# Loads in another order, the preparation of the second attention moved into the second step, and permutations copied by VectorE

## The chip, the cores and the metric

The kernel is written in Bass for one NeuronCore of one Trainium2 chip: every engine has its own instruction stream, written out by hand, and the streams wait for each other by semaphores. The metric is the device time of one execution in microseconds (us), and the number that counts is the median of several runs. A shorter time is better.

## The reference

Two layers on x of 16 batches x 128 rows x 128 columns, with a context of 16 batches x 77 rows x 128 columns. All is float32.

```python
x = x + tanh(g_xattn[0]) * L0_xattn(ctx, layernorm(x), mask, ...)   # 16 heads of 64, keys are [ctx rows, x rows]
x = x + tanh(g_ffn[0])   * L0_ffn(layernorm(x), ...)                # linear, 9 butterfly stages, gelu, 9 butterfly stages, linear
x = x + tanh(g_xattn[1]) * L1_xattn(layernorm(x), ctx, Wq, Wk, Wv, Wo, bq, bk, bv, bo)  # 16 heads of 8, top 32 of 77 keys
x = x + tanh(g_ffn[1])   * L1_ffn(layernorm(x), Wr, br, W1, W2)     # each row goes to one of 8 experts

# a butterfly stage, s = 2**stage: pairs i and i+s of the 512 hidden columns are mixed by a 2x2 matrix each
# second attention, what does not depend on x:
K = ctx @ Wk.T + bk ;  V = ctx @ Wv.T + bv ;  result @ Wo.T + bo
```

## The kernel before

**Stages.** A preparation, then a pipeline of steps over the 16 batches, then a last stage over 23 tiles of 128 rows sorted by expert. A step has eight slots (0 to 7). In one step six different batches are at work, each in another phase: P and A (first attention), A2 (its end and the butterfly FFN), B, C and E (second attention and router). Each engine has a function `step(i, at)` that lists its work slot by slot, so the order of work on an engine is fixed by hand. Steps 0 to 5 and the last ones are written out; the middle ones are one loop. Step 0 holds only the start of batch 0 (its P phase): POOL normalises the inputs (`stage_inputs`, semaphore p_step, slot 1), TensorE (PE) transposes them in slot 6 (`keys_T`), ScalarE (ACT) copies them out, and PE makes the first keys and queries (`keys_in`, `queries_in`). Step 1 is the first with scores, exponentials and attention.

**The preparation.** PE runs 15 jobs one after another: J_BIAS (transposed bias rows), J_BFT and J_BF (butterfly coefficients), J_WEXP (transposed W_exp), J_L1W (the four weights of the second attention transposed), J_CT (three jobs: the context transposed, line 718), J_K1 (three jobs: keys of the second attention, line 764), J_BO (line 768), J_V1 (four jobs: its values, line 775). Each fills one PSUM bank in turn; `move_jobs` copies it out, even jobs by ACT, odd jobs by VectorE (DVE). The copy J_BO waits for the DMAs of gates and bo (`ld_gates`, 48). Ahead of step 0, PE waits for the copies of the last eight jobs, and for Wq, both halves of Wkv, and Wout.

**Loads.** SyncE (SP) issues nearly all loads in one row, ACT issues the bias rows, the near butterfly weights and the four gains g1, g2, b1, b2, in that order. The rest of x (batches 1 to 15) is the twenty-fourth load of SP's row, behind gates and bo.

**Folding the butterfly.** The nine "up" stages are folded into W_exp and the nine "down" stages into W_con, one stage in a slot: POOL multiplies by the own coefficient (`up_part` line 572, `down_part` line 589), PE permutes (`up_perm` lines 985 and 987, `down_perm` line 993), DVE adds the two (`up_stage` line 1478, `down_stage` line 1504 or 1496), ACT does the bias column (`bias_stage`). The up stages stand in step 1, slots 0 to 7, and step 2, slot 0; the next one starts only when DVE and ACT are through. The down stages 8 and 7 stand in step 0, slots 5 and 6, and the others from step 1, slot 7. The permutation matrices `perm` are copies of the identity with halves exchanged, made by POOL (line 418) together with `spread` (line 420).

**Other lines that matter.** DVE takes the mean and variance of every input row (`input_stats`); `roots` on POOL makes 1/sqrt of them. `open_job(k)` waits for the copy of job k-8 and returns bank k mod 8. The bank names are GZ, TC, TL, OA, X, M and the two score banks S0 and S1.

```python
for k in range(JOBS - 8, JOBS):
    wait_job(pe, k)
for name in ("ld_wq", "ld_wk", "ld_wv", "ld_wout"):
    pe.wait_ge(s[name], 16)
```

## Time and profile before

| | us |
|---|---|
| median of 3 runs | 728.25 (727.86 to 730.04) |
| the profiled execution's own time | 727.75 |
| its span (first to last instruction) | 726.0 |
| PE busy | 648.3 (89%) |
| DVE busy | 571.3 (79%) |
| ACT busy | 482.0 (66%) |
| POOL busy | 448.7 (62%) |

Times inside the trace count from the start of the span. PE rows of float32 show two matmul records for one product, and a transpose shows one. A row of the timeline merges neighbours of one kind: its second number runs from the first start to the last end. The bracket at its end is the idle time before it and what ended it. "PEclk" is the clock that TensorE was granted, 1.00 for 2.4 GHz and 0.50 for 1.2 GHz.

### The profile page before, as it was taken

How to read it: one execution, taken by the hardware profiler on the slowest of the kernel's cores; microseconds unless marked ns; L12 is line 12 of the kernel's file. 1: busy time of each engine (PE TensorE's matmuls, PEld its weight loads, DVE VectorE, ACT ScalarE, POOL GpSimd, SP SyncE). 2: the span in 40 equal slices, each digit the busy share in tenths (PEclk: the TensorE clock that was granted, in tenths of full speed). 3: DMA queues.
4: the chain of work that ended last, by engine and by line, in shares of the span. 5: the costliest groups of instructions: out<-in, count | busy, mean ns of one | idle time of the engine just before them, and what ended most of it. 6: DMA issues, size and time to landing. Idle time of an engine off the chain costs nothing.

```text
span 726.0 us, 19295 instructions
## 1 busy us (share of the span) xinstructions
PE 648.3 (89%) x4994; PEld 528.0 (73%) x4994; DVE 571.3 (79%) x3740; ACT 482.0 (66%) x1331; POOL 448.7 (62%) x689
## 2 busy tenths in 40 slices
PE   6778999999999999999999999999999776771995
PEld 4646577778878786878787878778786755551995
DVE  3276639899999999898989899999999898943231
ACT  2266578787978788887878887978788533221231
POOL 8465677865767575757676575767675546543354
PEclk9799999999999999999999999999999855555898
DMA  7300079990000000000000000000000000003772
GB/s 208 75 1 1 1 201 296 325 282 4 2 2 1 1 1 0 0 0 0 0 0 0 0 0 0 0 0 0 0 1 2 1 0 30 30 23 102 213 225 61
DMA packets 38537, 37.92 MB, mean 52 GB/s; under 512 B 3633, under 2 KB 34249, under 8 KB 38484
## 3 DMA queue, kind: packets, MB, share of 16 engines
q1 hardware_dynamic: 32986, 27.76, 13.7%
q10 hardware_dynamic: 3994, 6.36, 3.0%
q0 software_dynamic: 1504, 3.17, 1.2%
q8 instruction: 24, 0.39, 0.2%
q14 instruction: 29, 0.24, 0.1%
HBM read 16.28 MB, written 21.45 MB: 52 GB/s over the span
## 4 chain that ended last, share of the span: by engine, by line
PE 48%; DVE 35%; issue 6%; POOL 3%; SPq 3%; DMA 2%; ACT 2%; DVEq 0%; another core or an unknown queue 0%; POOLq 0%
DVE sw L1566 14%; DVE m L1560 10%; PE bank L718 8%; PE bank L876 6%; PE bank L947 5%; PE bank L818 5%; PE bank L886 4%; DVE negmax L1513 3%; PE bank L1163 3%; PE score_banks L848 3%; PE bank L1173 3%; PE bank L828 2%; PE bank L806 2%; PE bank L910 2%; PE bank L901 2%
## 5 line engine op out<-in xcount | busy, mean ns | idle before, releaser
L1566 DVE MATCH_REPLACE8 sw<-m,sw 128x77 f32<-128x77 f32 x1024 | 219.8, 222 | 0.1
L1560 DVE MAX8 m<-sw 128x8 f32<-128x77 f32 x1024 | 188.9, 225 | 2.3 <-ACT sw L1191 1.3
L1191 ACT ACTIVATE prob<-score_banks,negmax 128x205 f32<-128x205 f32 x256 | 107.5, 433 | 22.1 <-DVE negmax L1513 22.1
L485 POOL TENSOR_TENSOR prob<-prob,inv 128x820 f32<-128x820 f32 x64 | 99.5, 1554 | 18.6 <-DVE inv L1518 18.6
L504 POOL TENSOR_TENSOR sw<-sw,m 128x616 f32<-128x616 f32 x64 | 78.0, 1218 | 50.0 <-DVEq L1547 49.7
L947 PEld LDWEIGHTS bank<-v,p1T 77*128 77x128 f32 x512 | 72.5, 216 | 15.6 <-DVE c_z L1592 5.2
L947 PE MATMUL bank<-v,p1T 77*128 (+1 forms) x512 | 72.3, 269 | 10.2 <-DVE c_z L1592 4.4
L1566 DVE MATCH_VALUE_LOAD sw<-m,sw 128x8 f32 x1024 | 76.9, 75 | 0.0
L1513 DVE TENSOR_REDUCE negmax<-score_banks 128x2 f32<-128x410 f32 x128 | 68.1, 573 | 2.7 <-PE score_banks L848 2.7
L718 PE MATMUL bank<-ident,prob 128*77 128x128 f32 (+1 forms) x512 | 67.3, 274 | 1.6 <-POOL prob L485 1.4
L828 PE MATMUL bank<-raw,kvT 128*77 128x512 f32 (+1 forms) x128 | 66.7, 603 | 0.0
L1191 ACT ACTIVATE h_ring<-bank 128x256 f32<-128x256 f32 (+1 forms) x87 | 38.5, 443 | 42.3 <-PE bank L1163 31.4
L718 PEld LDWEIGHTS bank<-ident,prob 128*77 128x77 f32 (+1 forms) x512 | 58.7, 146 | 9.3 <-POOL prob L485 5.2
L818 PE MATMUL bank<-kvT,raw 128*128 128x205 f32 x256 | 61.0, 362 | 1.2 <-DVE xs L1525 0.6
L930 PE MATMUL bank<-second_keys,b_q 128*128 128x308 f32 x128 | 53.2, 500 | 9.1 <-ACT p1T L1191 8.2
L848 PE MATMUL score_banks<-k_sb,q_sb 64*128 64x205 f32 x512 | 58.6, 348 | 0.0
L511 POOL TENSOR_TENSOR p<-sw 128x308 f32<-128x308 f32 x64 | 47.0, 735 | 18.0 <-ACT sw L1191 17.8
L876 PE MATMUL bank<-ptc,z_ring 77*64 77x128 f32 x512 | 53.1, 284 | 3.3 <-issue 2.6
L818 PEld LDWEIGHTS bank<-kvT,raw 128*128 128x128 f32 x256 | 43.7, 194 | 16.3 <-issue 14.5
L1191 ACT ACT_TABLE_LOAD x34 | 43.6, 1283 | 17.6 <-issue 17.0
L1191 ACT ACTIVATION_READ_ACCUMULATOR prob<-score_banks,negmax 128x1 f32 x256 | 53.0, 207 | 0.0
L1191 ACT ACTIVATE p1T<-bank 77x512 f32<-77x512 f32 x64 | 37.8, 591 | 19.7 <-PE bank L718 16.3
(235 smaller groups left out, 1457.4 us busy)
## 6 DMA issues: line engine op xcount, KB each, us to landing
z_sorted<-no_row SPq DMA_DIRECT2D x1, 17415.0 KB, 65.5
raw<-in_L_ffn_W ACTq DMA_DIRECT2D x23, 256.0 KB
z_ring<-z_sorted SPq DMA_DIRECT2D x23, 129.0 KB, 2.8
w<-in_L_ffn_W SPq DMA_DIRECT2D x8, 256.0 KB, 4.6
raw<-in_L_xattn_Wkv SPq DMA_DIRECT2D x2, 512.0 KB, 9.1
xs<-in_x SPq DMA_DIRECT2D x1, 960.0 KB, 6.9
cx<-in_ctx SPq DMA_DIRECT2D x1, 577.5 KB
raw<-in_L_xattn_Wq SPq DMA_DIRECT2D x1, 512.0 KB, 8.2
```

What stands on the lines that cost most here:

```text
L485: g.tensor_tensor(p, p, inv[:, 4 * q:4 * q + 4].unsqueeze(2).to_broadcast([128, 4, KV]), ALU.mult).then_inc(s["p_norm"], 1)
L504: g.tensor_tensor(v, v, m8[:, 4 * q:4 * q + 4, 0, 0:1].to_broadcast([128, 4, 2 * NK]), ALU.subtract).then_inc(s["sub_done"], 1)
L718: return nc.tensor.transpose(dst, src, ident[0:rows, 0:rows])
L818: last = mm(dst[:, KV * c:KV * c + KV], wkv_in[:, at:at + 128], kvT[:, :], start=True, stop=True)
L828: mm(dst[0:nr, :], kvT[:, r0:r0 + nr], wkv_in[:, INNER + 512 * j:INNER + 512 * j + 512], start=True, stop=True)\
L848: last = mm(SC[:, u, KV * r:KV * r + KV], q_sb[rows[u], q // 2, 2 * (q % 2) + r, :], k_sb[rows[u], q % 2, r, :], start=False, stop=(r == 1 ...
L876: last = mm(dst[64 * u:64 * u + 64, 128 * c:128 * c + 128], v[:, DH * h:DH * h + DH], p[:, 2 * c + u, :], start=not last_part, stop=last_p ...
L947: last = mm(M[:, c:c + D1 + 1], p1T[:, n, :], v1[:, bass.ds(b, 1), 4 * q + n, :].squeeze(1), start=True, stop=True)
L1191: return nc.scalar.activation(dst, src, f, **kw)
L1513: v.tensor_reduce(negmax[:, 2 * p:2 * p + 2], SC[:, :, KV * (p % 2):KV * (p % 2) + KV], AX_X, ALU.max, negate=True).then_inc(s["max_ready" ...
L1560: v.max(m8[:, h, r, :], sw[:, h, src, :]).then_inc(s[name], 1)
L1566: v.match_replace(sw[:, h, 1, :], m8[:, h, r, :], sw[:, h, src, :], TAKEN)\
```

## The change

1. **Loads.** SP's row becomes: x and ctx of batch 0, the mask, W_exp, Wq, the key half of Wkv, x of batches 1 to 3 (a semaphore of its own, `ld_near`), the weights of the second attention, the rest of ctx, gates and bo, the value half of Wkv, x of batches 4 to 15, W_con, far butterfly weights, Wout, the rest. ACT's row begins with the four gains, then the near butterfly weights, then the bias rows.
2. **POOL's constants.** The identity is finished right behind the first four fills; the mask rows, the ones of v1, the priorities, the empty row and the row numbers follow it. `perm` is no longer made by POOL: DVE copies it (14 copies, behind the mask rows and the copy of J_BFT). Both selections for `head_mask` move to step 0, slot 3, behind `coefficients`.
3. **Second attention.** J_L1W stays ahead of step 0. The three J_CT jobs come in step 0, slot 7; the J_K1 jobs in step 1, slots 0, 0, 1; J_BO in step 1, slot 1; the four J_V1 jobs in step 1, slots 2, 2, 2, 3. They use banks X, TC and TL, most of them TC, each waiting for the copy of the job before it in that bank.
4. **Waits.** Ahead of step 0, PE waits for the copies of J_BIAS and J_WEXP, and for Wq and the key half of Wkv. The value half is waited for in step 1, slot 2, Wout in step 2, slot 1. ACT waits for gates in step 0, slot 7, DVE for tanh(gates) in step 2, slot 0.
5. **Down stages** 8 and 7 move from step 0, slots 5 and 6, to step 1, slots 2 and 4; `roots(1, 4)` from step 0, slot 4, to step 1, slot 0. The input statistics of step 1 move from the start of their slots to the end.

The same products are computed on the same data. The diff, cut to its core:

```diff
+        JOB_BANK = [GZ, S0, S1, TC, X, X, TC, TL, X, TC, TC, TC, TC, TC, TC, TC]
-        DOWN_AT = {(0, 5): 8, (0, 6): 7}
+        DOWN_AT = {(1, 2): 8, (1, 4): 7}
 # POOL
-                for o in range(2):
-                    g.tensor_copy(p[:, :, o, :], q[:, :, 1 - o, :]).then_inc(s["c_perm"], 1)
                 w = 2 ** st
                 g.tensor_copy(spread[:, st, :]...
+            def head_blocks(): ...            # both affine_select of head_mask
                     if (i, slot) == (0, 3):
                         coefficients()
+                        head_blocks()
                     if slot == 0:
+                        if i == 1:
+                            roots(1, 4)
-                    if (i, slot) == (0, 4):
-                        roots(1, 4)
 # PE
             def open_job(k):
-                if k >= 8:
-                    wait_job(pe, k - 8)
-                return bank[k % 8]
+                for n in range(k):
+                    if JOB_BANK[n] is JOB_BANK[k]:
+                        before = n
+                if any(JOB_BANK[n] is JOB_BANK[k] for n in range(k)):
+                    wait_job(pe, before)
+                return JOB_BANK[k]
-            pe.wait_ge(s["c_perm"], 3 * PST)
+            pe.wait_ge(s["c_perm"], PST)
-            for k in range(JOBS - 8, JOBS):
-                wait_job(pe, k)
-            for name in ("ld_wq", "ld_wk", "ld_wv", "ld_wout"):
-                pe.wait_ge(s[name], 16)
+            second_weights_T()
+            wait_job(pe, J_BIAS)
+            wait_job(pe, J_WEXP)
+            pe.wait_ge(s["ld_wq"], 32)
 # PE, up_perm, st == 0
-                    pe.wait_ge(s["c_perm"], 3 * PST)
+                    wait_job(pe, J_K1)
+                    pe.wait_ge(s["c_odd"], PST + 1 + 2 * PST)
 # PE, step 0 slot 7 behind queries_in(P):   inputs_T(0), inputs_T(1), inputs_T(2)
 # PE, step 1 slot 0: keys_in(A, "GZ", 1); + second_keys_in(0); + second_keys_in(1)
 # slot 1: + second_keys_in(2); + wait_job(pe, J_CT + 2); keys_in(A, "TL", 2); + second_bias()
 # slot 2: + wait ld_wv; values_in(ctx); + second_values_in(0); scores(A, 1); + second_values_in(1);
 #         queries_in(A, "TL", 1); + second_values_in(2)
 # slot 3: values_in(lat); + second_values_in(3); keys_in(A, "GZ", 3); + wait_job(pe, J_V1 + 3); probs_T(A, 0)
 # ACT, step 0 slot 7: + my_jobs([J_CT + 1]), wait ld_gates, tanh
 # ACT, step 1: slot 0 end + J_K1; slot 1 ahead of exps(A, 0) + J_K1 + 2; slot 2 + J_V1;
 #              slot 3 behind queries_kept, ahead of exps(A, 2) + J_V1 + 2
 # DVE, ahead of step 0
-            my_jobs(range(1, J_L1W, 2))
-            dve.wait_ge(s["ld_c"], 16)
-            input_stats(1, 4, (1,))
-            my_jobs(range(J_CT, J_K1, 2))
-            dve.wait_ge(s["c_const"], 6 + NE)
+            dve.wait_ge(s["c_const"], 5)
             dve.wait_ge(s["ld_mask"], 32)
             ...                                # the two mask rows
-            my_jobs(range(J_K1 + 1, JOBS, 2))
-            dve.wait_ge(s["ld_x"], 16)
+            my_jobs([J_BFT])
+            for st in range(PST):
+                for o in range(2):
+                    v.tensor_copy(p[:, :, o, :], q[:, :, 1 - o, :]).then_inc(s["c_odd"], 1)
+            my_jobs([J_BF])
+            dve.wait_ge(s["ld_near"], 16)
             input_stats(1, 4, (0,))
 # DVE, step 0 slot 7: + my_jobs([J_CT]); wait ld_c; input_stats(1, 4, (1,)); my_jobs([J_CT + 2])
 # DVE, step 1: slot 0 + J_K1 + 1; slot 1 + J_BO; slot 2 end + J_V1 + 1; slot 3 + J_V1 + 3;
 #              input_stats(2 * slot + 2, 2 * slot + 4, (0, 1)) behind the slot's work; slot 1 waits ld_x
```

## Rows read from the trace of the kernel before

**Rows 1.** Stretches: length, busy us of PE, PEld, DVE, ACT, POOL; PEclk, DMA share, GB/s.

```profile
200.00:300.00 100.00, 97.96 (x816) 80.31 (x814) 92.35 (x641) 82.70 (x235) 66.54 (x91) 1.00 0.00 1
```

**Rows 2.** Timeline of PE, preparation and step 0: start, us, line, operation [idle before <-releaser].

```profile
7.07 0.25 PE L718 MATMUL bank<-ident,z_ring 11*128 11x11 f32 x1 [7.07 <-DMA z_ring<-in_L_ffn_down_weights]
...
11.94 1.11 PE L718 MATMUL bank<-ident,l_in 128*128 128x128 f32 x4
12.98 2.29 PE L718 MATMUL bank<-ident,cx 77*128 77x77 f32 x16
15.06 1.83 PE L764 MATMUL bank<-second_keys,l_wT 128*128 128x462 f32 x2
...
18.83 3.66 PE L775 MATMUL bank<-l_wT,second_keys 128*77 128x128 f32 x32
25.91 0.36 PE L718 MATMUL bank<-ident,p_ctx 77*128 77x77 f32 x1 [3.42 <-DVE v L320]
...
28.44 1.91 PE L806 MATMUL bank<-kvT,raw 128*128 128x128 f32 x8
```

**Rows 3.** Timeline of DVE, the end of the preparation.

```profile
15.70 2.09 DVE L1466 TENSOR_SCALAR mask_rows<-mask_u 1x1232 bf16<-1x1232 uint8 x2
...
23.74 0.29 DVE L1429 TENSOR_TENSOR bo<-bo,bank 128x128 f32<-128x128 f32 x1 [4.75 <-DMA bo<-in_L_xattn_bo]
```

**Rows 4.** Timeline of the two issuing queues, SP and ACT.

```profile
19.55 0.43 SPq L364 DMA_DIRECT2D bo<-in_L_xattn_bo  x1
...
3.02 0.41 ACTq L1202 DMA_DIRECT2D z_ring<-in_L_ffn_down_weights  x1
...
4.37 0.93 ACTq L1205 DMA_DIRECT2D b<-in_L_xattn_b  x2
```

**Rows 5.** DMA issues: KB each, median us from issue to landing.

```profile
b<-in_L_xattn_b ACTq DMA_DIRECT2D x2, 64.0 KB, 7.8
...
gates<-in_g_ffn SPq DMA_DIRECT2D x1, 1.0 KB, 2.4
```

**Rows 6.** Timeline of POOL, from the roots of batch 0 to the first butterfly product.

```profile
11.74 0.55 POOL L449 TENSOR_TENSOR rs_c<-rs_c,half 77x1 f32<-77x1 f32 x1
13.87 0.40 POOL L474 TENSOR_TENSOR p_ctx<-cx,ln_c 77x128 f32<-77x128 f32 x1 [1.58 <-DMA b<-in_L_xattn_b]
...
15.72 0.45 POOL L474 TENSOR_TENSOR p_lat<-p_lat,g 128x128 f32<-128x128 f32 x1
16.13 1.00 POOL L474 TENSOR_TENSOR p_ctx<-p_ctx,b 77x128 f32<-77x128 f32 x1
...
35.93 1.05 POOL L572 TENSOR_TENSOR wu_t<-wu,bf_own 128x516 f32<-128x516 f32 x1
```

**Rows 7.** Timeline of PE in step 1: first scores, waits, and the next step's scores.

```profile
31.29 0.32 PE L843 MATMUL score_banks<-mask_now,ones_rows 64*128 64x154 bf16 x2 [0.93 <-ACT q_sb L1191]
31.37 1.68 PE L848 MATMUL score_banks<-k_sb,q_sb 64*128 64x205 f32 x8
...
39.05 1.10 PE L985 MATMUL bank<-wu,perm 128*128 128x512 f32 x2 [2.35 <-DVE wu L1478]
...
40.12 1.06 PE L828 MATMUL bank<-raw,kvT 128*77 128x512 f32 x2
42.91 0.24 PE L843 MATMUL score_banks<-mask_now,ones_rows 64*128 64x154 bf16 x2 [1.72 <-ACT prob L1191]
...
50.14 0.90 PE L848 MATMUL score_banks<-k_sb,q_sb 64*128 64x205 f32 x8
...
69.25 0.24 PE L843 MATMUL score_banks<-mask_now,ones_rows 64*128 64x154 bf16 x2
```

**Rows 8.** Timeline of DVE in step 1, slots 5 and 6: a stage waiting for PE.

```profile
60.15 1.13 DVE L1478 SCALAR_TENSOR_TENSOR wu<-bank,bf_cross,wu_t 128x128 f32<-128x128 f32 x4 [2.21 <-PE bank L985]
```

**Rows 9.** Stretches of PE: length, busy, PEclk, DMA share, GB/s.

```profile
29.00:30.00 1.00, 1.00 (x7) 0.50 0.00 0
...
35.00:36.00 1.00, 1.00 (x5) 1.00 0.00 0
```

More of the change, by code:

```diff
@@ L685, in step @@
                         if A2 is not None:
+                            if i == 2:
+                                for k in range(J_K1, J_BO):
+                                    wait_job(pool, k)
                             spread_keys(A2)
@@ L747, in _, with second_weights_T, inputs_T @@
             last.then_inc(s["set_psum"], 1)
[L748 to L755 removed]
+            def second_weights_T():
+                pe.wait_ge(s["ld_l1w"], 64)
+                dst = open_job(J_L1W)
+                for n in range(4):
+                    last = turn(dst[:, 128 * n:128 * n + 128], l1_in[:, n, :])
+                last.then_inc(s["set_psum"], 1)
+            def inputs_T(k):
+                if k == 0:
+                    pe.wait_ge(s["ld_first"], 32)
+                    pe.wait_ge(s["ld_c"], 16)
+                b0, nb = CT_PART[k]
                 dst = open_job(J_CT + k)
@@ L759, in _, with second_keys_in @@
                 last.then_inc(s["set_psum"], 1)
-            wait_job(pe, J_L1W)
-            for k, (b0, nb) in enumerate(CT_PART):
+            def second_keys_in(k):
+                b0, nb = CT_PART[k]
+                wait_job(pe, J_L1W)
                 wait_job(pe, J_CT + k)
@@ L765, in _, with second_bias, second_values_in @@
                     .then_inc(s["set_psum"], 1)
-            wait_job(pe, J_BIAS)
-            dst = open_job(J_BO)
-            mm(dst[:, 0:D], bv.to_broadcast([128, 128]), l1_wT[:, 3, :], start=True, stop=True)\
-                .then_inc(s["set_psum"], 1)
-            for k in range(NB // 4):
+            def second_bias():
+                wait_job(pe, J_BIAS)
+                dst = open_job(J_BO)
+                mm(dst[:, 0:D], bv.to_broadcast([128, 128]), l1_wT[:, 3, :], start=True, stop=True)\
+                    .then_inc(s["set_psum"], 1)
+            def second_values_in(k):
                 dst = open_job(J_V1 + k)
@@ L1126, in step @@
                             queries_in(P, "OA", 0, 0, 2)
+                            if i == 0:
+                                for k in range(3):
+                                    inputs_T(k)
                         if A is not None:
@@ L1200, in _, with my_jobs @@
                 at += n
-            for a, name in enumerate(("L0_ffn_up_weights", "L0_ffn_down_weights")):
-                act.dma_start(bf_rows[PST * HC * a:PST * HC * (a + 1), :],
-                              t[name][0:PST].rearrange("s (c k) a b -> (s c) (k a b)", c=HC)).then_inc(s["ld_bias"], 16)
-            for dst, name in ((g1, "L0_xattn_g1"), (g2, "L0_xattn_g2"), (b1, "L0_xattn_b1"), (b2, "L0_xattn_b2")):
-                act.dma_start(dst[:, :], row(name)).then_inc(s["ld_gain"], 16)
-            move_jobs(act, range(0, JOBS, 2), copy, lambda d, v, b: fn(d, v, ACT.Identity, bias=b))
-            act.wait_ge(s["ld_gates"], 48)
-            fn(tg[:, :], gates[:, :], ACT.Tanh).then_inc(s["c_gate"], 1)
+            def my_jobs(jobs):
+                move_jobs(act, jobs, copy, lambda d, v, b: fn(d, v, ACT.Identity, bias=b))
+            my_jobs(range(0, J_CT, 2))
             def keys_out(b):
@@ L1395, in step @@
                             queries_kept(P, OA, 0, 2)
+                            if i == 0:
+                                my_jobs([J_CT + 1])
+                                act.wait_ge(s["ld_gates"], 48)
+                                fn(tg[:, :], gates[:, :], ACT.Tanh).then_inc(s["c_gate"], 1)
                         if C is not None:
@@ L1673, in step @@
                         down_stage(DOWN_AT[before])
+                    if (i, slot) == (0, 7):
+                        my_jobs([J_CT])
+                        dve.wait_ge(s["ld_c"], 16)
+                        input_stats(1, 4, (1,))
+                        my_jobs([J_CT + 2])
+                    if (i, slot) == (2, 0):
+                        dve.wait_ge(s["c_gate"], 1)
                     if (i, slot) == (2, 2):
@@ L1682, in step @@
                         row_places(0 if i == 17 else 1)
-                    if i == 1 and 1 <= slot <= 6:
-                        input_stats(2 * slot + 2, 2 * slot + 4, (0, 1))
                     if slot == 0:
@@ L1698, in step @@
                         top_first(C, 7)
+                        if i == 1:
+                            my_jobs([J_BO])
                     if slot == 2:
@@ L1754, in step @@
                             residual(A2, batch(xs, A2), GZ[:, 0:D], 2, "x2_ready")
-            dve.wait_ge(s["c_gate"], 1)
+                    if i == 1 and 1 <= slot <= 6:
+                        if slot == 1:
+                            dve.wait_ge(s["ld_x"], 16)
+                        input_stats(2 * slot + 2, 2 * slot + 4, (0, 1))
             run_steps(dve, step)
```

106 lines of the change are left out of this document (72 added, 34 removed).

## The prediction

> **What bounds the kernel now.** I read the table of stretches first. In the middle of the run PE is busy 97.96 of 100 us at the full clock, and DVE 92.35 [rows 1]. The change leaves that work alone, so whatever the start gains moves the whole pipeline forward by as much, and whatever step 1 loses moves it back. The pipeline waits for nothing that keeps an absolute time: the clearing of the sorted buffer hangs on the folding of the weights and moves with it. So the question is one of two dates: when step 1 begins and when step 2 begins.
>
> The timeline of PE gives both. The first job starts at 7.07, when the last of the seven bias and coefficient DMAs has landed. The jobs follow one another to 22.5. Then PE waits 3.42 us, and `keys_T` of batch 0 starts at 25.91 [rows 2]. The wait is put down to a DVE copy of v. The timeline of DVE says what held that copy: the J_BO addition sat 4.75 us behind the DMA of bo, and DVE's two copies of v, which PE needs, stand behind it in `move_jobs` [rows 3]. SP issued bo only at 19.55, after 3.5 MB of other loads [rows 4]. POOL had finished the inputs of batch 0 at 18.1 (17.10 plus 1.00; two operations of 1.00 from 16.13) [rows 6]. So 7.8 us of the start are preparation and loads that batch 0 doesn't need. Step 1 begins at 31.29, step 2 at 69.25, and so step 1 lasts 38.0 us [rows 7].
>
> **The change, part by part: the date of keys_T.** PE keeps the jobs up to and with J_L1W. They took from 7.07 to 13.05 (11.94 + 1.11), 6.0 us [rows 2]; waits for `spread` were already all but hidden, and now it is earlier. These durations hold again, since this is PE's first work after the start in both kernels.
>
> What moves is their beginning. ACT issues the four gains first, so the last bias row is issued at about 5.1, where the last gain was before (4.37 + 0.93 ends at 5.30) [rows 4]. Before, the last one needed was issued at 3.02 and released PE at 7.07, 4.05 us later. I take the same 4.05 us: 9.1. Bounds: 2.4 us, the shortest landing (a 1 KB load) gives 7.5; the longer of the two landings of b (their median is 7.8; the slower one, issued at 4.84, released POOL at 13.87, so 9.0 us) gives 14.1 [rows 4 to 6]. PE is then through at 9.1 + 6.0 = 15.1.
>
> POOL must be ready too. The roots of batch 0 ended at 12.3 (11.74 + 0.55) [rows 6]. Ahead of them 14 perm copies (0.20 us from one to the next, 2.9 us) go away, so 9.4. The eight operations of `stage_inputs` took from 13.87 to 18.1. Six took 2.3 us in all (13.87 to 15.72 + 0.45), and the last two 1.00 each instead of 0.45; without that it is 3.2 us, so POOL is ready at 12.6, or 13.7 with it. The gains, issued 2.65 us sooner, land at 13.87 - 2.65 = 11.2 at the latest, which gives 14.4. All of these are under 15.1: PE's own jobs set the date, and POOL has 0.7 to 2.5 us to spare.
>
> The perm copies go to DVE, behind the copy of J_BFT, at about 10 to 12.5, where DVE has nothing else to do until J_BF is ready. Their price there has no row; a quarter to one times POOL's 0.2 us each gives 0.7 to 2.9 us, hidden in both cases behind PE's J_BF and J_L1W. They do run beside `stage_inputs` on POOL, and the row that speaks to this is POOL's 1.00 instead of 0.45, exactly while DVE's two mask operations ran from 15.70 to 17.79 [rows 3, 6]. Priced by that row, 2.9 us of copies cost POOL 2.9 us at most: 12.6 becomes 15.5, 0.4 us beyond PE. I leave it at nothing and keep the 0.4.
>
> The Trainium skill, "SBUF — State Buffer", section "Who interferes with whom", says that a VectorE copy that uses both ports and a GpSimd operation exclude each other for the whole instruction. The doubled POOL operations agree with it. By that rule alone each perm copy may hold POOL for its own length, which is the 0.4 us bound again.
>
> Loads for step 0: Wq and the key half of Wkv are now fifth and sixth in SP's row. Before, they stood behind 0.8 MB more and were there long before 25.9. They fall under 15.1 with ease. So **keys_T at 15.2**, 10.7 us sooner.
>
> **From keys_T to step 1.** Transposes, copy, first keys, first queries took from 25.91 to 30.35 (28.44 + 1.91), 4.45 us at the granted clock 0.50 [rows 2, 9]. PE will be no warmer this time. Its first jobs ran at the lower rate too, whatever the clock column says there: a J_K1 product of 462 columns took 1.83 us at 15.06, one of 512 columns 1.06 us at 40.12, and the J_V1 products from 18.83 on are back at the full rate (32 records 0.11 apart) [rows 2, 7]. That is 11.5 us of work from 7.07 to the full rate; now the first keys come 7 us behind the first job. So 4.45 stays, and step 1, 13 us behind the first job, has the full clock. Behind them the change puts the three J_CT jobs, 2.29 us [rows 2]. Their banks are free by then. The wait for q_sb (0.93) is hidden behind them. Step 1 begins at 15.2 + 4.45 + 2.3 = 21.95, against 31.29: **9.3 us sooner**.
>
> **Step 1 itself** gets seven us of foreign work, and here I walk slot by slot.
> Slots 0 and 1 lasted 31.29 to 40.12, 8.8 us [rows 7]. Of that, 1.6 us were the low clock (scores 1.68 against 0.90 at 50.14, keys the same again), which ended at 35 [rows 7, 9]. Another 2.35 us were the wait for DVE's first stage, late because POOL had `roots(1, 4)` and two down products ahead of its first up product, at 35.93 [rows 6, 7]. After the change POOL does this product as soon as the coefficients are there, near 18, so that wait goes. What comes instead: three J_K1 jobs, by the same two rows about 0.8 us at the full rate for 462 columns and 0.5 for the short one, 2.1 together; J_BO, 0.2; and four waits in a row, as the jobs share bank TC (each copy about 0.65 us on ACT or DVE, plus 0.2 us hand-over), of which I find about 1.3 us uncovered. -1.6 - 2.35 + 2.1 + 0.2 + 1.3 = -0.3.
> Slots 2 and 3 lasted 40.12 to 50.1, 9.9 us. They get the four J_V1 jobs, 3.66 us, already at the full rate [rows 2]. The first is covered. The second waits for ACT's copy of the first, behind `bias_stage` and two other copies: 0.6. The fourth waits for ACT's copy of the third, behind `bias_stage`: 1.3; against that, the 1.72 us that PE waited for ACT ahead of these slots' scores is now filled with work [rows 7]. And `down_stage(8)` on DVE ahead of J_V1+3, 1.1 us, runs while PE makes the fourth job. 3.7 + 0.6 + 1.3 - 1.7 = +3.9.
> Slots 4 to 7: one more down product on POOL (1.05) and `down_stage(7)` on DVE (1.9) in slot 5. DVE waited 2.21 us for PE right there [rows 8]. That is the cover, and if it were gone the cost would be up to 1.9. I take 0. The input statistics at the end of the slots move nothing that PE waits for.
> Step 1 therefore lasts 38.0 - 0.3 + 3.9 = 41.6, **3.6 us longer**. Bounds: +1.0, if the PE work is half absorbed by waits it had anyway, and +5.5 with the DVE cover gone.
>
> The rest costs nothing: `head_blocks` and the coefficients end near 18 and are first used in step 1 or 2; rest of ctx and x, the value half, W_con and Wout are needed at 19.5, 26, 30, 31 and 65, while before the last of all the loads landed at 26.9 with the same bytes in the row.
>
> **Sum.** Step 2 begins 9.3 - 3.6 = 5.7 us sooner. The profiled execution took 727.75 by its own time, 0.5 below the median of 728.25, and so 722.05 or, from the median, **722.5 us**.
>
> **Rivals.**
> *Late bias rows.* The gains (256 KB in 512 packets) now stand ahead of the bias rows that PE's first job waits for. For it: one b took 9.0 us to land. Against: then SP's row was full of small packets of ctx, now it begins with large ones. Taking 12.5 for the first job: 3.4 us later, 725.9; at 14.1, 727.5. From 14.8 on the gain is gone. [...]
> *The moved work fully exposed (the slower side).* The eight jobs of step 1 form one chain through bank TC: PE, copy, PE. If nothing covers it, it costs 2.1 + 0.2 + 3.7 us of PE, eight copies of 0.6 and eight hand-overs of 0.2, 12.4 us in all, against the 9.3 gained: 731.4. It decides from 9.3 us on. For it: copies stand in ACT's and DVE's queues behind butterfly stages, whose POOL, PE, ACT round trip already paces the slots. Against: other PE work lies between any two of the jobs.
> *PE stays at the low clock into step 1.* The dense stretch that ended at 22.5 becomes a short one with gaps. For it: after 3.4 us of waiting the clock stood at 0.50 until 35 [rows 2, 9]. Slots 0 and 1 would then keep their 1.6 us and pay 2.3 more for the J_K1 and J_BO jobs: +3.9, 726.4.
> *It moves nothing.* What is gained is only waited for again in steps 2 and 3, by the down stages: 728. Against: they are paced from PE to DVE in the same step, not by a date.
>
> **How the numbers follow.** Forecast 0.58 (718.3 to 724.4: the first job at 7.5 and step 1 only 1.0 longer, or step 1 5.5 longer); late bias rows 0.15; low clock 0.10; nothing moved 0.07; exposed 0.10. A measurement tells about 0.3%, 2.2 us, from no change, so faster means under 726.0. Faster: 0.58, two thirds of the late rows, half of the low clock, 0.03 of the rest, 0.76. Slower than 730.4: 0.10. Same: 0.14. The range takes in the low clock and the late rows at 14.1 with step 1 another 1.0 us longer, 728.5, and below 718.0. It leaves out the exposed chain and part of the case in which nothing moves.
>
> **What would show it.** PE's first job near 9.1; `keys_T` near 15.2 with no wait of over a microsecond ahead of it, and no DMA of bo there; first scores near 22.0; L985 first near 25 and POOL's first up product long before it; step 2's first scores near 63.5. In slots 2 and 3, waits of PE for ACT's and DVE's v copies of under 2 us in all. The prediction is wrong if the first job starts after 12, if `keys_T` waits for POOL's p_lat, or if step 1 lasts over 44 us.

## The result, and the profile after

The changed kernel took 723.82 us (median of 9 runs, 722.79 to 726.56), the kernel before in the same comparison 729.5 us. The ratio is 0.9931 with a 95% interval of 0.9914 to 0.9947, about 5.0 us (3.9 to 6.3). The profiled executions took 723.82 and 727.75 us, with spans of 722.1 and 726.0.

The first 100 us of before and, under it, of after (length, busy us of PE, PEld, DVE, ACT, POOL, then PEclk, DMA share, GB/s):

```profile
0.00:100.00 100.00, 79.73 (x506) 57.03 (x507) 50.56 (x184) 49.80 (x155) 62.03 (x132) 0.95 0.22 60
```

```profile
0.00:100.00 100.00, 81.52 (x550) 59.04 (x551) 55.45 (x204) 52.41 (x161) 64.20 (x124) 1.00 0.28 75
```

PE has 44 more matmul records in the same 100 us, and the granted clock no longer falls. The timeline of PE after, the rows that answer to [rows 2, 7]:

```profile
11.84 0.25 PE L726 MATMUL bank<-ident,z_ring 11*128 11x11 f32 x1 [11.84 <-DMA z_ring<-in_L_xattn_bv]
...
16.71 1.11 PE L726 MATMUL bank<-ident,l_in 128*128 128x128 f32 x4
17.62 0.34 PE L726 MATMUL bank<-ident,p_ctx 77*128 77x77 f32 x1
...
20.27 1.92 PE L832 MATMUL bank<-kvT,raw 128*128 128x128 f32 x8
21.98 2.12 PE L726 MATMUL bank<-ident,cx 77*128 77x77 f32 x16
24.03 0.24 PE L869 MATMUL score_banks<-mask_now,ones_rows 64*128 64x154 bf16 x2
...
25.74 1.72 PE L785 MATMUL bank<-second_keys,l_wT 128*128 128x462 f32 x4
27.46 1.10 PE L1012 MATMUL bank<-wu,perm 128*128 128x512 f32 x2
...
31.64 1.06 PE L854 MATMUL bank<-raw,kvT 128*77 128x512 f32 x2
...
34.95 1.10 PE L801 MATMUL bank<-l_wT,second_keys 128*77 128x128 f32 x8 [0.46 <-ACT v L1243]
...
41.03 1.10 PE L801 MATMUL bank<-l_wT,second_keys 128*77 128x128 f32 x8 [1.16 <-ACT v L1243]
...
44.92 0.24 PE L869 MATMUL score_banks<-mask_now,ones_rows 64*128 64x154 bf16 x2
...
64.19 0.24 PE L869 MATMUL score_banks<-mask_now,ones_rows 64*128 64x154 bf16 x2
```

The row at 17.62 is `keys_T`: it comes 8.3 us sooner than in [rows 2], with no wait ahead of it. Step 1 begins at 24.03 (31.29 before) and step 2 at 64.19 (69.25 before), 5.06 us sooner. From there the shift doesn't change: the scores that start at 197.40 before start at 192.34 after, 5.06 again. The last stage begins 5.13 us sooner (671.40 and 666.27), but lasts to the end of the span 55.8 instead of 54.6 us, and so the spans differ by 3.9. That tail lasted between 53.9 and 55.8 us in all the kernels below, with no relation that I see to what was changed. I take the date of step 2 as the measure and leave the tail aside: in the twelve profiled executions the time of the execution minus its date of step 2 was 658.3 to 659.8 us. So two dates of step 2 that differ by less than about 1.5 us need not mean two different times.

**A second date.** From these rows alone it looks as if the step from 25.91 to 17.62 had been the gain. The rows of DVE say otherwise. DVE's part of the first butterfly up stage is called S0 from here on (it is not the score bank of that name). It is the last row of the first fence, which is the kernel before, and the row of the second, which is after:

```profile
26.95 0.68 DVE L1452 BATCH_NORM_STATS2 st<-xs 128x6 f32<-128x128 f32 x3 [1.72 <-DMA xs<-in_x]
...
33.71 1.14 DVE L1504 SCALAR_TENSOR_TENSOR wd<-wd,bf_far,wd_t 128x128 f32<-128x128 f32 x4 [5.74 <-POOL wd_t L589]
...
37.84 1.11 DVE L1478 SCALAR_TENSOR_TENSOR wu<-bank,bf_cross,wu_t 128x128 f32<-128x128 f32 x4
```

```profile
28.68 1.12 DVE L1545 SCALAR_TENSOR_TENSOR wu<-bank,bf_cross,wu_t 128x128 f32<-128x128 f32 x4 [0.48 <-PE bank L1012]
```

Before, a chain beside PE leads to S0: the x of the batches 1 to 15 lands at 26.95, DVE's statistics, POOL's `roots(1, 4)` (28.06 to 32.5), two down products with their DVE stages (32.55 to 37.8), S0 at 37.84. PE was through with its part of the stage, which S0 needs as well, at 35.90 (35.62 + 0.28), so that this chain held S0 by 1.9 us. PE in the kernel before:

```profile
35.62 0.28 PE L987 MATMUL bank<-wu,perm 128*128 128x4 f32 x2
```

After, x of batches 1 to 3 is there early, the down stages are behind S0, and DVE waits for PE's L1012: now PE's own order of work, from `keys_T` on, releases S0. S0 comes 9.16 us sooner, step 2 only 5.06. The 4.10 us between them are what the change put behind S0. The experiments ask which of the two dates paces the start, and which part of the change buys what.

### The profile page after: what moved, and what is told of

It reads as the page before. It is cut to its first block, busy times and chain, and to the rows that moved or that the text cites. A ratio compares the mean times of both kernels' runs of the same rounds, so it can differ in the third digit from the quotient of the medians.

```text
span 722.1 us, 19294 instructions
## 1 busy us (share of the span) xinstructions
PE 645.1 (89%) x4994; PEld 525.4 (73%) x4994; DVE 574.9 (80%) x3754; ACT 481.7 (67%) x1331; POOL 445.9 (62%) x675
## 3 DMA queue, kind: packets, MB, share of 16 engines
q0 software_dynamic: 1504, 3.17, 1.2%
## 4 chain that ended last, share of the span: by engine, by line
PE 50%; DVE 35%; issue 5%; POOL 2%; ACT 2%; DMA 2%; ACTq 1%; DVEq 0%; another core or an unknown queue 0%; SPq 0%; POOLq 0%
DVE sw L1633 14%; DVE m L1627 10%; PE bank L726 8%; PE bank L902 6%; PE bank L844 5%; PE bank L973 5%; PE bank L912 4%; DVE negmax L1580 3%; PE bank L1215 3%; PE score_banks L874 3%; PE bank L1225 3%; PE bank L854 2%; PE bank L832 2%; PE bank L936 2%; PE bank L927 2%
## 5 line engine op out<-in xcount | busy, mean ns | idle before, releaser
L1243 ACT ACTIVATE sw<-sw 128x616 f32<-128x616 f32 x64 | 46.9, 733 | 5.7 <-POOL sw L507 5.4
```

The costliest lines, as they stand in the source:

```text
L1243: return nc.scalar.activation(dst, src, f, **kw)
```

## The experiments

The dates of all the runs in one table, in us from the start of each profiled execution, read from the rows that answer to those above: PE's first instruction, `keys_T` of batch 0, the first scores of step 1, S0, the first scores of step 2. "Ratio" is against the kernel before in the same comparison.

| kernel | first job | keys_T | step 1 | S0 | step 2 | S0 to step 2 | median | ratio |
|---|---|---|---|---|---|---|---|---|
| before | 7.07 | 25.91 | 31.29 | 37.84 | 69.25 | 31.41 | 729.5 | |
| after | 11.84 | 17.62 | 24.03 | 28.68 | 64.19 | 35.51 | 723.82 | 0.9931 |
| e1 | 7.14 | 17.45 | 22.62 | 27.27 | 62.77 | 35.50 | 722.57 | 0.9903 (0.9883 to 0.9923) |
| e2 | 7.33 | 15.08 | 21.63 | 26.27 | 61.77 | 35.50 | 720.67 | 0.9885 (0.9861 to 0.9910) |
| e3 | 12.33 | 18.10 | 23.61 | 28.25 | 63.76 | 35.51 | 723.68 | 0.9931 (0.9903 to 0.9960) |
| e4 | 12.60 | 18.38 | 24.68 | 31.66 | 66.69 | 35.03 | 727.22 | 0.9962 (0.9946 to 0.9977) |
| e5 | 5.93 | 25.50 | 29.70 | 36.17 | 67.59 | 31.42 | 727.35 | 0.9972 (0.9956 to 0.9988) |
| e6 | 6.47 | 24.73 | 29.63 | 34.94 | 66.35 | 31.41 | 726.18 | 0.9965 (0.9947 to 0.9982) |
| e7 | 12.98 | 18.76 | 24.37 | 28.27 | 60.94 | 32.67 | 720.45 | one run |
| e8 | 6.91 | 17.19 | 23.74 | 30.29 | 65.79 | 35.50 | 722.94 | 0.9899 (0.9859 to 0.9940) |
| e9 | 6.23 | 19.40 | 25.09 | 29.74 | 65.25 | 35.51 | 726.10 | 0.9952 (0.9931 to 0.9972) |
| e10 | 7.08 | 24.58 | 28.17 | 31.05 | 62.73 | 31.68 | 723.15 | 0.9909 (0.9879 to 0.9939) |

The column to read is "S0 to step 2". It is 31.41 or 31.42 in the three kernels with the work of before, and 35.50 or 35.51 in the six with the moved jobs and the moved down stages, while `keys_T` moves by 4.3 us among these six. From the start of step 1 to step 2 there are 40.14 to 40.16 us in five of the six and 42.05 in e8, 37.96 us in before and 36.72 in e6. Where the two differ, step 2 goes by S0. This says what follows S0, not what sets it. In before, e5 and e6 the chain through x ended last; PE was through with its part 1.9, 1.5 and 2.5 us sooner. In the other nine kernels PE's row ends right ahead of S0 (DVE waits 0.47 or 0.48 us for PE's permutation in seven of them), so there the date of `keys_T` and what PE does or waits for behind it set S0.

**e1, the order of ACT's loads.** Bias rows, near weights, gains, as before; all else as after.

```diff
-            for dst, name in ((g1, "L0_xattn_g1"), (g2, "L0_xattn_g2"), ...): act.dma_start(...)
-            for a, name in enumerate(("L0_ffn_up_weights", "L0_ffn_down_weights")): act.dma_start(...)
             ...                                # the bias rows
+            for a, name in enumerate(("L0_ffn_up_weights", "L0_ffn_down_weights")): act.dma_start(...)
+            for dst, name in ((g1, "L0_xattn_g1"), (g2, "L0_xattn_g2"), ...): act.dma_start(...)
```

> The changed kernel with one edit: ACT issues the bias rows and near butterfly weights first and the four gains last, as the kernel before does. In the changed kernel PE's first job started at 11.84 us, keys_T at 17.62, step 2 at 64.19. Theory (the gains ahead of the bias rows in ACT's queue made the first job late, and both loads are needed at once): first job back at 7.1 to 8, PE through with its jobs at about 13.5, but the gains land near 13.9 as before the change, POOL is ready at 17.1, keys_T at 17.2; step 2 at 63.8, the time within 0.5 us of the changed kernel. Rival A (only the first job mattered, the gains land soon enough with SP's new row): keys_T at 14, step 2 at 60.5, 3.6 us faster than the changed kernel. Rival B (the order in ACT's queue is not what made it late, SP's row is): first job still past 11, nothing moves.

The first job is back at 7.14: ACT's order alone made it late. `keys_T` gains nothing from it. The timeline of PE in e1, and under it that of POOL:

```profile
7.14 0.25 PE L726 MATMUL bank<-ident,z_ring 11*128 11x11 f32 x1 [7.14 <-DMA z_ring<-in_L_ffn_down_weights]
...
14.60 1.11 PE L726 MATMUL bank<-ident,l_in 128*128 128x128 f32 x4 [2.53 <-DMA l_in<-in_L_xattn_Wo]
17.45 0.36 PE L726 MATMUL bank<-ident,p_ctx 77*128 77x77 f32 x1 [1.73 <-POOL p_lat L477]
...
21.45 1.23 PE L726 MATMUL bank<-ident,cx 77*128 77x77 f32 x16
```

```profile
14.19 0.40 POOL L477 TENSOR_TENSOR p_ctx<-cx,ln_c 77x128 f32<-77x128 f32 x1 [3.60 <-DMA b<-in_L_xattn_b]
```

PE waits for a weight load and then for POOL, which waits 3.60 us for the gains. Two paths of almost the same length meet at `keys_T`, and taking one of them back leaves the other. Still, step 2 comes 1.4 us sooner than after. The difference is in the last PE row: the sixteen transposes of cx take 1.23 us here and 2.12 after, and the first queries ahead of them 1.63 instead of 1.92. With the 0.17 us at `keys_T` that is the 1.4. PE was at its full rate sooner (sixteen such transposes take 1.23 us at it and 2.12 to 2.29 at the low one, whatever the clock column says so early). That the edit did this isn't shown: e3 has the loads of after and the late first job, and its transposes of cx took 1.23 us too.

**e2, the gains on SP.** Bias rows first on ACT, and the four gains in SP's row right behind ctx of batch 0; ACT's lines for them go.

```diff
             sp.dma_start(cx[:, 0, :], t["ctx_1024"][0]).then_inc(s["ld_first"], 16)
+            for dst, name in ((g1, "L0_xattn_g1"), (g2, "L0_xattn_g2"), ...):
+                sp.dma_start(dst[:, :], row(name)).then_inc(s["ld_gain"], 16)
```

> The changed kernel with one edit: the four gains are issued by SP right behind x and ctx of batch 0, and ACT issues only the bias rows and near butterfly weights. Theory (the first job hangs on ACT's queue, POOL's inputs on the gains): first job at 7.1 to 8, gains land before 10, POOL is ready at 13.5, PE is through with its jobs at 13.5 to 14; keys_T at 13.7, step 1 at 20, step 2 at 60.2, about 4 us faster than the changed kernel and 9 faster than the kernel before (ratio 0.987). Rival (the two queues share one issue path, so moving loads between them moves nothing): first job still past 10, at most 1 us faster.

Now both paths are short: `keys_T` at 15.08, step 2 at 61.77, 2.4 us sooner than after. It is the fastest kernel here with all of the work in it, and its interval (0.9861 to 0.9910) lies below that of after. It missed its own expectation by 1.4 us at `keys_T`, because the gains pushed W_exp back. PE in e2, and then DVE's perm copies in e1 and in e2:

```profile
9.64 1.12 PE L728 MATMUL score_banks<-ident,w_exp 128*128 128x128 f32 x4 [1.54 <-DMA w_exp<-in_L_ffn_W_exp]
```

```profile
8.36 1.55 DVE L1534 COPY perm<-ident 128x64 f32<-128x64 f32 x14
```

```profile
10.96 3.69 DVE L1534 COPY perm<-ident 128x64 f32<-128x64 f32 x14
```

In e1 POOL works on its small 128x1 operations meanwhile and then waits for the gains; in e2 it runs the operations of `stage_inputs`. The same 14 copies cost 1.55 and 3.69 us. They cost 1.52 to 1.55 where POOL ran none of those operations beside them (e1, e4, e8), 3.69 again in e9 and 3.17 in e7, where it did, and 1.90 in after, where only the last one overlapped; those of POOL stayed at 0.39 to 0.45 us. So the two engines do hold each other up, but with these short copies DVE paid, not POOL as I had priced it. Beside a long DVE operation it was POOL: the first operation of `stage_inputs`, 0.40 us elsewhere, took 0.96 in e2 while DVE made the mask rows. The Trainium skill, "SBUF — State Buffer", section "Who interferes with whom", says that it is the order of issue that decides who waits. Rows in which once DVE and once POOL pays fit that; which of two single operations was issued first wasn't read.

**e3, the permutations back on POOL.** Everything else as after.

```diff
+                for o in range(2):             # POOL, ahead of each copy of spread
+                    g.tensor_copy(p[:, :, o, :], q[:, :, 1 - o, :]).then_inc(s["c_perm"], 1)
-                    v.tensor_copy(p[:, :, o, :], q[:, :, 1 - o, :]).then_inc(s["c_odd"], 1)   # DVE
```

> The changed kernel with one edit: the 14 perm copies are back on POOL, beside the spread copies. Theory (POOL had slack, it was ready with the inputs of batch 0 at 13.5 and PE at 17.6): POOL's inputs come 2.9 us later, at 16.4, still ahead of PE; keys_T, step 2 and the time stay within 0.3 us of the changed kernel. Rival (POOL is on the path): keys_T up to 2.9 us later and so is everything behind it, step 2 at 67.

POOL has the inputs of batch 0 at 16.03 instead of 13.49, and PE needs them at 18.10: `keys_T` stands as far behind the first job (5.77 us) as after (5.78). Ratio 0.9931, like after. This part of the change is worth nothing that can be measured here.

**e4, the down stages back in step 0.**

```diff
-        DOWN_AT = {(1, 2): 8, (1, 4): 7}
+        DOWN_AT = {(0, 5): 8, (0, 6): 7}
```

> The changed kernel with one edit: down stages 8 and 7 are back in step 0, slots 5 and 6. In the changed kernel they cost DVE 1.95 us each in step 1, slots 2 and 4, and I had counted them at nothing, covered by waits for PE. Theory (they are covered in step 1, while in step 0 POOL and DVE must wait for W_con and the far weights, which land past 20 us, with up_part(0), roots and the J_CT copies queued behind): step 1's first stage is later by 2 to 4 us, step 2 at 65 to 67, 1 to 3 us slower than the changed kernel. Rival (they cost their full length in step 1): step 2 at 61 to 63, 1 to 3 us faster.

Step 2 comes 2.5 us later, more than in any other run that takes back one thing. But 0.65 us of that was there at the start of step 1 (24.68 against 24.03), with a first job at 12.60, which this edit doesn't touch; step 1 itself is 1.85 us longer (42.01 against 40.16). POOL in e4, DVE, then PE:

```profile
22.65 1.05 POOL L593 TENSOR_TENSOR wd_t<-wd,bf_far 128x512 f32<-128x512 f32 x1 [2.25 <-DMA bf_far<-in_L_ffn_down_weights]
24.95 1.04 POOL L593 TENSOR_TENSOR wd_t<-wd,bf_far 128x512 f32<-128x512 f32 x1 [1.25 <-DVE wd L1571]
25.95 1.05 POOL L576 TENSOR_TENSOR wu_t<-wu,bf_own 128x516 f32<-128x516 f32 x1
```

```profile
26.02 1.94 DVE L1571 SCALAR_TENSOR_TENSOR wd<-wd,bf_far,wd_t 128x128 f32<-128x128 f32 x4 [1.16 <-POOL wd_t L593]
27.88 0.63 DVE L311 COPY second_keys<-bank 128x462 f32<-128x462 f32 x1
```

```profile
28.65 1.79 PE L785 MATMUL bank<-second_keys,l_wT 128*128 128x462 f32 x4 [2.10 <-DVE second_keys L311]
```

POOL reaches the down products 2.25 us before the far weights land, DVE's down stages wait for POOL, and DVE's copy of the first J_CT job stands behind them. PE waits 2.10 us for that copy ahead of J_K1, and its part of the first up stage comes behind J_K1, so that S0 comes at 31.66 instead of 28.68. (POOL's first up product, ready at 27.00, was early enough.) Behind S0 the step is 0.48 us shorter without them: that is what the down stages cost in their new place, by this pair; e6 and e10 give 0.27.

**e5, e6, e10: from the kernel before, loads and down stages alone.** e5 puts gates and bo ahead of Wq in the old kernel. e6 does that and loads x of batches 1 to 3 by itself behind them. e10 is e6 with the two down stages in step 1. None of the three moves any preparation.

```diff
 # e5, e6, e10
+            sp.dma_start(gates[:, 0:2], row("g_xattn")).then_inc(s["ld_gates"], 16)
+            sp.dma_start(gates[:, 2:4], row("g_ffn")).then_inc(s["ld_gates"], 16)
+            sp.dma_start(bo[:, :], row("L1_xattn_bo")).then_inc(s["ld_gates"], 16)
 # e6, e10
+            sp.dma_start(xs[:, 1:4, :], t["x"][1:4].rearrange("b s d -> s b d")).then_inc(s["ld_near"], 16)
             sp.dma_start(wq_in, t["L0_xattn_Wq"]).then_inc(s["ld_wq"], 16)
-            dve.wait_ge(s["ld_x"], 16)         # ahead of step 0; now in step 1, slot 1
+            dve.wait_ge(s["ld_near"], 16)
 # e10
-        DOWN_AT = {(0, 5): 8, (0, 6): 7}
+        DOWN_AT = {(1, 2): 8, (1, 4): 7}
```

> The kernel before with one edit: the three small loads gates, gates and bo are issued ahead of Wq instead of behind the far butterfly weights. It takes away the one wait to which the trace puts keys_T's late date. My reading in the prediction (PE's wait for the v copies is what held the start): keys_T at 23.3 instead of 25.91, no fall of the clock to 0.50, so step 1 begins near 27 and step 2 3 to 5 us sooner than at 69.25, near 65: most of the gain of the whole change. Rival (a second path ends almost as late: x of batches 1 to 3 lands at 26.95, then DVE's statistics, POOL's roots until 32.5 and two down products until 36 stand ahead of the first butterfly product): step 1 begins sooner but its slot 1 waits longer, step 2 stays at 68.5 to 69.3 and the time within 1 us.

> The run with gates and bo ahead of Wq, and behind them, still ahead of Wq, the load of x of batches 1 to 3 split off from the rest of x. The preparation, the permutations and the down stages stay as in the kernel before. Theory (two late paths, both by loads): x of batches 1 to 3 is there before the jobs end, the statistics end at 24.3, the roots at 28.6, the two down products at 32; first butterfly stage at 33.5 instead of 37.84, step 2 at about 65: 4 us gained, almost as much as the whole change. Rival (the moved preparation is what gains, the order of the loads is only needed for it): step 2 at 67 or later.

> The kernel before with three small edits: gates and bo ahead of Wq, x of batches 1 to 3 split off behind them (as in the run that had this, first stage at 34.94, step 2 at 66.35), and now down stages 8 and 7 in step 1, slots 2 and 4, as in the changed kernel. The whole preparation of the second attention stays ahead of step 0, the permutations stay on POOL. In that run POOL had the roots at 29.6 and PE its first permutation at 32.5, and only the two down stages on POOL and DVE held the first butterfly stage until 34.94. Theory (step 2 hangs on the first butterfly stage, not on the first scores or on the length of the preparation): first stage at 32.6, step 2 31.4 us and the 0.5 us of the down stages' new place later, at 64.5, as early as the whole change brings it (64.19), with the time within 1 us of the changed kernel. Rival (the moved preparation is worth its own gain): step 2 no earlier than 66.

e5 takes away the DMA of bo, on which the prediction laid the wait of 3.42 us [rows 2, 3]. `keys_T` comes only 0.4 us sooner (25.50): PE's own preparation ended at 24.10 (20.32 plus 3.78) instead of 22.49, since the J_K1 products took 2.77 us instead of 2.08 and PE waited 0.61 us for the rest of ctx ahead of them. But S0 comes 1.67 us sooner and step 2 1.66 us: the x that was issued behind bo came 1.67 us sooner too. From DVE's statistics of x to S0 it is 10.89 us in before (26.95 to 37.84) and in e5 (25.28 to 36.17), and 10.86 in e6 (24.08 to 34.94). Neither of the two expectations for e5 (3 to 5, or 0 to 0.7) fits; the chain through x does. e6 brings S0 to 34.94 and step 2 to 66.35, so these loads alone give 2.90 us, less than the 4 that were expected.

e10 is the run that says what the moved preparation is worth. With `keys_T` at 24.58, 7 us later than after, it reaches step 2 at 62.73, 1.46 us sooner. DVE in e10, then PE, then POOL:

```profile
31.05 1.12 DVE L1479 SCALAR_TENSOR_TENSOR wu<-bank,bf_cross,wu_t 128x128 f32<-128x128 f32 x4 [6.11 <-PE bank L986]
```

```profile
26.18 1.05 PE L807 MATMUL bank<-kvT,raw 128*128 128x128 f32 x8
...
30.74 0.28 PE L988 MATMUL bank<-wu,perm 128*128 128x4 f32 x2
```

```profile
28.59 0.84 POOL L450 TENSOR_TENSOR rs_c<-rs_c,half 77x3 f32<-77x3 f32 x1
29.51 1.04 POOL L573 TENSOR_TENSOR wu_t<-wu,bf_own 128x516 f32<-128x516 f32 x1
```

The roots no longer have anything behind them but the up product, which is ready at 30.55, and PE is through with its part at 31.02: the two paths to S0 end 0.5 us apart, PE's last. Nothing but the two down stages came behind S0: 31.68 us to step 2.

The run was expected at 32.6 for S0 and 64.5 for step 2, and both came 1.6 to 1.8 us sooner. PE in e6, which differs from e10 only in the two down stages, shows why:

```profile
26.79 1.91 PE L807 MATMUL bank<-kvT,raw 128*128 128x128 f32 x8
...
32.20 0.28 PE L988 MATMUL bank<-wu,perm 128*128 128x4 f32 x2
```

In e6 the granted clock fell to 0.50 between 26 and 29, in e10 it stayed at 1.00, and so PE's part of the first up stage ended at 31.02 instead of 32.48. The edit isn't the cause: in e6 POOL begins the down stages only at 29.66. From `keys_T` to that end it is 6.44 us in e10 and 7.75 in e6, so that 1.3 us of e10's date are the clock. As an estimate from these rows, e10 with e6's clock has S0 at about 32.3 and, 31.7 us later, step 2 at 64.0, close to the 64.19 of after.

The median of e10, 723.15, can't be told from that of after (0.9879 to 0.9939 against 0.9914 to 0.9947). So three small edits, with all the preparation ahead of batch 0, do what the whole change does, by that estimate with either clock.

**e9, the moved work with the old loads.** Both rows of loads as before, but x still in two parts.

> The changed kernel with both rows of loads in the order of the kernel before (x of batches 1 to 3 stays a load of its own, at the old place of x). So it is the moved work alone. All runs so far have step 2 beginning a fixed time behind DVE's first butterfly stage: 31.4 us in the kernels with the old preparation, 35.5 with the moved one. Theory (the two parts of the change add up through that date): x of batches 1 to 3 lands at 26.9, DVE's statistics of it stand ahead of its J_CT copies, these at 28 to 30, J_K1 behind them, first butterfly stage at 31.6, step 2 at 67.1: 2 us gained. Rival (the move needs no load order): first stage at 28 to 29, step 2 at 64.

PE in e9 ahead of `keys_T`:

```profile
15.39 3.17 PE L756 MATMUL bank<-bf_k,spread 64*128 64x32 f32 x14 [7.36 <-DVE bf_k L302]
```

DVE waited for the mask until 13.21, and the copy of J_BFT stands behind it: 7.36 us of PE. S0 comes at 29.74 all the same, and step 2 4.0 us sooner than before, at 65.25, between the two expectations (67.1 and 64). The expectation had x of batches 1 to 3 land at 26.9 and S0 at 31.6; cut off from the other 12 batches, x had landed by 24.5. The loads of e6 alone give 2.9, the moved work with x split 4.0, the whole change 5.06: the parts don't add up, since they bring forward the same S0.

**e7, the moved jobs made tiny.** The four J_V1 and three J_K1 jobs compute and copy 8 columns each instead of all; the result of the second attention is left out.

```diff
-                mm(dst[:, 0:nb * NK], l1_wT[:, 1, :], cT[:, b0 * NK:(b0 + nb) * NK], ...)
+                mm(dst[:, 0:8], l1_wT[:, 1, :], cT[:, b0 * NK:b0 * NK + 8], ...)
-                for n in range(4): ...         # J_V1: four products of 128 columns
+                last = mm(dst[0:NK, 0:8], cT[:, 4 * k * NK:(4 * k + 1) * NK], l1_wT[:, 2, 0:8], ...)
```

> The changed kernel with the moved J_K1 and J_V1 jobs cut to 8 columns each, product and copy, at the same places and with the same waits (J_K1 makes 8 columns of its keys, J_V1 8 columns of one batch's values, the rest of both is filled with constants by POOL ahead of the roots; so the result of the second attention is not computed). It prices the foreign work in step 1, which lasts 40.16 us in the changed kernel and lasted 38.0 before. Theory of the prediction (the jobs cost their PE time and some waits for copies, 6 us, less the waits they fill): step 1 at 34.5 to 35.5. Rival (what lengthens step 1 is the chain of hand-overs through bank TC, not the size of the work): step 1 at 38 to 40.

Step 1 lasts 36.57 us instead of 40.16, and from S0 to step 2 it is 32.67 instead of 35.51, in one run. Of the 4.10 us behind S0, 2.84 are thus the size of these jobs, 0.48 the down stages (e4), and about 0.8 are left for the hand-overs, J_BO and the rest, which I didn't separate. The result lies between the two expectations: the step took 1.1 us more than one and 1.4 less than the other.

**e8, W_exp ahead of the mask and the gains.** An attempt to mend e2's wait of 1.54 us.

```diff
+            sp.dma_start(w_exp[:, :], t["L0_ffn_W_exp"]).then_inc(s["ld_wexp"], 16)
             ...                                # mask, then the four gains, then Wq
```

> The run with the gains on SP's queue, where W_exp was waited for 1.54 us by PE at 9.64 and the copy of J_BFT 0.32 us: now SP issues W_exp right behind x and ctx of batch 0, then the mask, then the four gains. Theory: PE's jobs end at 13.4 to 13.6, POOL's inputs at 13.5, keys_T at 13.7 instead of 15.08, step 1 1.4 us sooner at 20.2 if the clock rises at the same distance, step 2 at 60.4 instead of 61.77. Rival (the gains now land later and POOL becomes the bound): keys_T at 15 or later, nothing gained.

```profile
16.28 1.11 PE L728 MATMUL bank<-ident,l_in 128*128 128x128 f32 x4 [4.44 <-DMA l_in<-in_L_xattn_Wo]
```

The wait for W_exp went, and one of 4.44 us for the second attention's weights came in its place; step 2 at 65.79 is worse than in after. That is not the wait: `keys_T` at 17.19 and step 1 at 23.74 are both ahead of after. PE in e8, the first scores of step 1:

```profile
23.85 1.66 PE L876 MATMUL score_banks<-k_sb,q_sb 64*128 64x205 f32 x8
```

They took 0.90 us in after. PE was at the low rate until past 27, and S0 stood 6.55 us behind the start of step 1 instead of 4.65. `keys_T` is 2.1 us later than in e2, so the edit shows no gain; what it costs isn't told by one trace. Its four executions took 719.78 to 725.13 us, the profiled one being the slowest, and with the same rows of loads the first job came at 11.84, 12.33, 12.60 and 12.98 in after, e3, e4 and e7. e2 stays the best.

## Why the prediction came out right, and where its reasons did not

The time was forecast at 722.5 us and came at 723.82, the gain at 5.7 us and came at 5.06 in the trace. By its own steps:

- **First job, 9.1; it came at 11.84.** The last bias row was to be issued at 5.1 and was issued at 6.72, since ACT's issues stretched (below), and it took 5.1 us from there to the release of PE instead of 4.05. The bound of 14.1 held. Here the forecast had luck: it named a first job after 12 as the sign of being wrong, and e3, e4 and e7, with the same rows of loads, have it at 12.33 to 12.98.
- **PE's jobs, 6.0 us:** 11.84 to 17.82 (16.71 + 1.11). Right. POOL was ready at 13.49, by 12.6 to 14.4 in the forecast, and had over 4 us to spare instead of 0.7 to 2.5, because PE was late.
- **keys_T, 15.2; it came at 17.62,** with no wait ahead of it, as said.
- **From keys_T to step 1, 6.75 us; it took 6.41.** Step 1 began 2.1 us later than forecast. e1 takes the late bias rows back, 4.7 us of the first job, and wins 1.4 us of step 1, 1.2 of it by the rate: the weights and the gains are then the next waits. So the rival of the late bias rows was true of the first job and nearly void for `keys_T`.
- **Slots 0 and 1: -0.3; -1.2.** They took 7.61 us (24.03 to 31.64) instead of 8.8. The wait of 2.35 us went as said.
- **Slots 2 and 3: +3.9; +3.3.** 31.64 to 44.92 is 13.28 us against 9.94 (40.12 to 50.06). PE waited 0.46 and 1.16 us for ACT's v copies, 1.6 in all, under the 2 that I had named.
- **Slots 4 to 7: 0; +0.1.** The down stage is covered, as taken. e4 prices both stages at 0.48, e10 at 0.27.
- **Step 1, 41.6; it took 40.16.** It became 2.2 us longer, not 3.6. This error of 1.4 us and the late start of 2.1 us had opposite signs, so that step 2 was off by only 0.6: that the total came so near is luck.
- **Permutations on DVE, 0.7 to 2.9 us, hidden:** 1.90 us, and hidden. That POOL would pay up to 2.9 us for them was the wrong way round (e2).
- **The clock.** I kept the low rate for the first keys and the full one for step 1, and so it was: the cx transposes still took 2.12 us for sixteen, the scores at 24.11 took 0.90. The fall to 0.50 at about 25 to 35 [rows 9] is gone with the wait.

What did not hold is the step at the top: "7.8 us of the start are preparation and loads that batch 0 doesn't need", read as what holds the start, with the wait of 3.42 us laid on the DMA of bo. e5 takes that DMA away and `keys_T` gains 0.4 us. The chain through x, the roots and the down products was in the prediction as the cause of a wait of 2.35 us in slot 1, and as a price that was about right: it held S0 1.9 us longer than PE did. But because it ended last in the kernel before, `keys_T` alone coming sooner would have left S0 where it was; x, the roots and the down stages had to move for it to count. Once they are moved, PE's path, the one the prediction walks, sets S0 again, in after and in e10.

Read so, the change's parts weigh differently. S0 goes from 37.84 to 31.05 with the loads and the two down stages alone (e10, 6.8 us, of which 1.3 are the clock of that execution and 0.27 are given back behind S0). With the second attention's preparation moved too, S0 is at 28.68, 2.4 us sooner, and 3.8 us are paid behind it (35.51 - 31.68): PE's work has only changed places. In the dates of step 2 that is a loss of 1.5 us, about as much as the clock gave e10; in the medians it can't be told from nothing.

Two things stay open. How the last 0.8 us behind S0 divide was not tried. And the date at which PE reaches its full rate isn't decided by the first job alone: e3 (first job at 12.33) had the cx transposes at 22.44 in 1.23 us, after (11.84) at 21.98 in 2.12. It was worth 0.9 us between these two, 1.9 in e8, and 1.3 between e6 and e10, where the granted clock fell in e6, and I have no cause for it. It is why e3, with `keys_T` 0.48 us later than after, has step 2 0.43 us sooner.

## What to carry to other kernels

Before costing the removal of a wait, look for the date at which the next stage hangs: walk back from an engine's first piece of the paced work (here a DVE stage) along everything that it needs, not only from the longest wait on the busiest engine, and compare over two or three variants which path ended last. Before comparing two dates, look at the rate at which the busiest engine worked on the way to them: here it was worth as much as most of the edits. Where two paths meet with almost equal lengths, as `keys_T` did in e1, shortening one buys the difference and no more. Try the small edits first: here a load split off and sent early and two stages put behind the critical one gave as much as moving the preparation of a whole attention layer, and the best single addition to the whole change was to send the four gains (256 KB) on the other queue.

## What the runs showed of the hardware that was not expected

**Issuing a DMA has no fixed duration.** ACT's queue after and then SP's:

```profile
3.76 1.52 ACTq L1256 DMA_DIRECT2D z_ring<-in_L_ffn_b_exp  x1
...
6.72 0.43 ACTq L1256 DMA_DIRECT2D z_ring<-in_L_xattn_bv  x1
```

```profile
3.63 1.97 SPq L352 DMA_DIRECT2D xs<-in_x  x1
...
8.89 3.54 SPq L356 DMA_DIRECT2D gates<-in_g_xattn  x1
```

The issue of b_exp took 0.57 us as the first of ACT's row before and 1.52 us behind gains and near weights, while SP's issue of x took 1.97 us at the same time; that the one lengthens the other was not tested. A load of 1 KB took 3.54 us to issue behind the rest of ctx; in e1 the same one took 6.12. The bytes of the load being issued don't explain it. Whether what stands ahead of it in its queue does was not tested alone. Landing moved likewise: b took 8.2 us from issue to landing behind the bias rows in ACT's queue (e1), 5.2 ahead of them (after) and 5.1 in SP's (e2).

**The clock fell behind a short wait in two kernels, and not in a third.** In e5 and e6 the wait ahead of `keys_T` was only 1.40 and 1.29 us instead of 3.42, and the granted clock went down all the same; in e10 the wait was 1.29 again, and it stayed at 1.00. PE's stretches in e5 and, in the second fence, in e10 (length, busy, PEclk, DMA share, GB/s):

```profile
25.00:30.00 5.00, 3.13 (x18) 0.74 0.02 4
30.00:35.00 5.00, 5.00 (x20) 0.58 0.00 0
```

```profile
25.00:30.00 5.00, 3.69 (x27) 1.00 0.01 3
30.00:35.00 5.00, 3.95 (x15) 1.00 0.01 2
```

In e5 PE had its full clock ahead of the wait and lost it behind it, and the mean stayed below 1.00 while PE was busy without a gap from 30 to 35. What decides between the two is open.
